# Pre-FFN normalisation and quantisation: statistics taken once for all 16 token tiles, and the rounding moved from VectorE to ScalarE

## The reference

```python
def act_quant(x):
    scale = 127.0 / jnp.clip(jnp.max(jnp.abs(x), axis=-1, keepdims=True), 1e-05)
    return jnp.clip(jnp.round(x * scale), -128, 127) / scale

def _L0_ffn_ref(x, w1, conv_w, conv_b, w2):
    h = bit_linear(x, w1)                      # act_quant(x) @ weight_quant(w1).T
    h = depthwise_conv1d(h.transpose(0, 2, 1), conv_w, conv_b)
    h = jax.nn.silu(h.transpose(0, 2, 1))
    return bit_linear(h, w2)

# x: [16, 2048, 1024] f32, hidden 4096
x = x + _L0_attn_ref(_layernorm(x), ...)
x = x + _L0_ffn_ref(_layernorm(x), w1, conv_w, conv_b, w2)
```

## Time and profile before

| what | value |
|---|---|
| runs of the kernel before | 4776.62 and 4817.77 us, median 4797.2 |
| profiled execution: time | 4801.58 us |
| profiled execution: span of its slowest core (core 0) | 4800.0 us |
| spans of the eight cores | 4755.6 to 4800.0 us |
| busy on core 0: PE / DVE / ACT | 2736.8 / 1853.6 / 964.5 us |
| C-prep of the first sequence on core 0 | 1697.3 to 1819 us |
| C-prep of the second sequence on core 0 | 3802 to 3923 us |

### The profile page before, as it was taken

The page is one execution under the profiler, slowest core; times in us unless marked ns, Lnnn a source line. Parts: engine busy times, 40 slices in busy tenths (PEclk is TensorE's granted clock), DMA queues, the critical chain, the costliest instruction groups (busy, mean ns, idle before and its releaser), DMA issues. The chain is left out here.

```text
span 4800.0 us, 49252 instructions; the slowest of 8 cores (4755.6 to 4800.0 us)
## 1 busy us (share of the span) xinstructions
PE 2736.8 (57%) x16882; PEld 1410.7 (29%) x17064; DVE 1853.6 (39%) x4571; ACT 964.5 (20%) x1070; POOL 45.5 (1%) x68
## 2 busy tenths in 40 slices
PE   0166546677721216768785466456777536768675
PEld 0022113333311114444442122123333224444342
DVE  1121144332323365646554212243222465545643
ACT  0011013455511101111110010025446201101010
POOL 0000000000000000000000000000000000000000
PEclk9999756656555558989898798755665669989888
DMA  7500012111154303444454300000000013544444
GB/s 128 162 27 18 18 68 76 68 62 45 36 156 125 130 9 71 115 136 141 128 153 135 124 19 17 18 18 10 18 18 1 9 27 71 149 114 147 122 136 149
DMA packets 472114, 380.92 MB, mean 79 GB/s; under 512 B 340674, under 2 KB 373570, under 8 KB 466756
## 3 DMA queue, kind: packets, MB, share of 16 engines
q1 hardware_dynamic: 460612, 335.81, 23.9%
q0 software_dynamic: 11264, 41.95, 2.7%
HBM read 335.77 MB, written 41.94 MB: 79 GB/s over the span
## 5 line engine op out<-in xcount | busy, mean ns | idle before, releaser
L80 ACT ACTIVATE b_pt<-b_lp,b_cb 128x1024 bf16<-128x1024 f32 (+3 forms) x640 | 622.9, 985 | 626.2 <-PE b_lp L80 394.7
L80 PE MATMUL c_op<-c_w2b,c_hq 128*128 128x512 bf16 x2032 | 516.8, 400 | 256.3 <-DMA c_w2b<-w2t_s 182.5
L80 PE MATMUL b_av<-V,b_pt 128*128 128x65 bf16 x5120 | 383.7, 241 | 336.6 <-DVE b_pt L80 240.7
L80 PE MATMUL c_hp<-c_xq,c_w1b 128*128 128x257 bf16 x4096 | 525.1, 284 | 66.9 <-ACT c_H L80 58.3
L80 PEld LDWEIGHTS b_av<-V,b_pt 128*128 128x128 bf16 x5120 | 296.9, 125 | 633.5 <-issue 633.5
L80 PEld LDWEIGHTS c_hp<-c_xq,c_w1b 128*128 128x128 bf16 x4096 | 411.2, 101 | 205.3 <-issue 104.6
L80 ACT ACTIVATE c_H<-c_hp,c_cb 128x512 bf16<-128x512 f32 x256 | 175.9, 687 | 1243.3 <-DVE c_H L80 647.2
L80 PE MATMUL b_lp<-Q,K 64*128 64x512 bf16 x1280 | 375.0, 602 | 11.0 <-DVE x L80 9.3
L80 PEld LDWEIGHTS c_op<-c_w2b,c_hq 128*128 128x128 bf16 x2048 | 198.0, 101 | 552.1 <-issue 359.8
L80 DVE TENSOR_TENSOR c_H<-c_hp,c_g1b 128x514 bf16<-128x514 f32 x256 | 176.7, 690 | 462.2 <-PE c_hp L80 462.1
L80 DVE TENSOR_TENSOR b_pt<-b_pt,c_tri 128x128 bf16<-128x128 bf16 x512 | 92.7, 222 | 626.8 <-ACT b_pt L80 626.6
(11 more groups left out here) (119 smaller groups left out, 2256.7 us busy)
## 6 DMA issues: line engine op xcount, KB each, us to landing
c_w2b<-w2t_s SPq DMA_DIRECT2D x256, 512.0 KB, 5.2
c_w1b<-w1t_s SPq DMA_DIRECT2D x128, 512.0 KB, 4.3
pw_stg<-w SPq DMA_DIRECT2D x32, 1024.0 KB, 4.8
wq_stw<-w SPq DMA_DIRECT2D x16, 2048.0 KB, 9.1
a_xt<-x SPq DMA_DIRECT2D x32, 512.0 KB, 3.7
b_xr<-x SPq DMA_DIRECT2D x32, 512.0 KB, 3.5
out<-c_obf POOLq DMA_DIRECT2D x32, 512.0 KB, 3.1
wq_s<-p_wbf POOLq DMA_DIRECT2D x16, 512.0 KB, 8.0
```

The costliest lines, as they stand in the source:

```text
L80: h = getattr(eng, en["name"])(*en["args"], **en["kwargs"])
```

## The change

Everything between the two memsets of c_xq and the barrier is rewritten:

- Statistics are taken for all 16 token tiles before the group loop: 32 `bn_stats` (into the new tile c_pb), 16 `bn_aggr` (c_mw), and one chain of addition, square root, reciprocal and Newton step on 128x16 values of the new tile c_cq instead of four chains on 128x4 values. The new tiles take 1408 bytes of each partition.
- In each group VectorE keeps the four normalisations, the four maxima and the four small steps to the scale. Two waits are added ahead of the normalisations from the second group on (for the transposes and the roundings of the group before); for the transposes it waited before.
- The eight rounding instructions go to ScalarE as `activation` with `AF.Identity`: the first with a 128x1 scale and a 128x1 bias (MAGIC), the second with a 128x1 bias (-MAGIC). They are issued in pairs: first rounding of tiles 0 and 1, a ScalarE drain, second rounding of tiles 0 and 1, then the same for tiles 2 and 3.
- TensorE no longer waits for the whole group's rounding but for that of the one tile (`sc_r2[u]`).

TensorE's instructions are the same in number and order. The diff, cut where the small steps repeat:

```diff
@@ -791,85 +791,104 @@
                 nc.sbuf_tensor(f"c_xv{s}", [128, 4 * D], F32, side="right"))
             cxm = es_cp.enter_context(
                 nc.sbuf_tensor(f"c_xm{s}", [128, 4 * D], BF16, side="right"))
+            cpb = es_cp.enter_context(
+                nc.sbuf_tensor(f"c_pb{s}", [128, 192], F32, side="right"))
+            mv16 = es_cp.enter_context(
+                nc.sbuf_tensor(f"c_mw{s}", [128, 32], F32, side="right"))
+            cs2 = es_cp.enter_context(
+                nc.sbuf_tensor(f"c_cq{s}", [128, 128], F32, side="right"))
             ve.inc(r.vector.memset(
                 xq2.rearrange("p (c t) -> p c t", c=8)[:, :, 0:1], 0.0))
             ve.inc(r.vector.memset(
                 xq2.rearrange("p (c t) -> p c t", c=8)[:, :, S + 1:S + 2], 0.0))
             tn_pq = [0] * NT
             ve_pq = [0] * NT
-            var_s = mvc.rearrange("p (j two) -> p two j", two=2)[:, 1:2, :]
+            sc_r2 = [0] * NT
+            sc_r1 = [0] * NT
+            for u in range(NT):
+                ve.inc(r.vector.bn_stats(cpb[:, u * 12:u * 12 + 6],
+                                         x2[:, u * D:u * D + 512]))
+                ve.inc(r.vector.bn_stats(cpb[:, u * 12 + 6:u * 12 + 12],
+                                         x2[:, u * D + 512:(u + 1) * D]))
+            ve.inc(r.vector.drain())
+            for u in range(NT):
+                ve.inc(r.vector.bn_aggr(mv16[:, u * 2:(u + 1) * 2],
+                                        cpb[:, u * 12:u * 12 + 12]))
+            ve.inc(r.vector.drain())
+            var16 = mv16.rearrange("p (j two) -> p two j", two=2)[:, 1:2, :]
+            ve.inc(r.vector.tensor_scalar_add(
+                cs2.rearrange("p (a b) -> p a b", a=1)[:, :, 0:16], var16,
+                EPS))
+            r.wait(r.scalar, ve)
+            sc.inc(r.scalar.activation(cs2[:, 16:32], cs2[:, 0:16], AF.Sqrt))
+            r.wait(r.vector, sc)
...
+            ve.inc(r.vector.tensor_mul(cs2[:, 64:80], cs2[:, 32:48],
+                                       cs2[:, 48:64]))
+            ve.inc(r.vector.drain())
             for tq in range(NT // 4):
+                q0 = 4 * tq
+                if tq >= 1:
+                    r.wait(r.vector, tn, tn_pq[q0 - 1])
+                    r.wait(r.vector, sc, sc_r1[q0 - 1])
                 for j in range(4):
-                    u = 4 * tq + j
-                    ve.inc(r.vector.bn_stats(bnsc[:, j * 12:j * 12 + 6],
-                                             x2[:, u * D:u * D + 512]))
-                    ve.inc(r.vector.bn_stats(bnsc[:, j * 12 + 6:j * 12 + 12],
-                                             x2[:, u * D + 512:(u + 1) * D]))
-                ve.inc(r.vector.drain())
-                for j in range(4):
-                    ve.inc(r.vector.bn_aggr(mvc[:, j * 2:(j + 1) * 2],
-                                            bnsc[:, j * 12:j * 12 + 12]))
-                ve.inc(r.vector.drain())
-                ve.inc(r.vector.tensor_scalar_add(
-                    cst.rearrange("p (a b) -> p a b", a=1)[:, :, 0:4], var_s,
-                    EPS))
-                r.wait(r.scalar, ve)
-                sc.inc(r.scalar.activation(cst[:, 4:8], cst[:, 0:4], AF.Sqrt))
...
-                if tq >= 1:
-                    r.wait(r.vector, tn, tn_pq[4 * tq - 1])
-                for j in range(4):
-                    u = 4 * tq + j
+                    u = q0 + j
                     ve.inc(r.vector.tensor_scalar(
                         cxt[:, j * D:(j + 1) * D], x2[:, u * D:(u + 1) * D],
-                        mvc[:, 2 * j:2 * j + 1], cst[:, 16 + j:17 + j],
+                        mv16[:, 2 * u:2 * u + 1], cs2[:, 64 + u:65 + u],
                         ALU.subtract, ALU.mult))
                 ve.inc(r.vector.drain())
                 for j in range(4):
-                    ve.inc(r.vector.reduce_max(cst[:, 20 + j:21 + j],
+                    u = q0 + j
+                    ve.inc(r.vector.reduce_max(cs2[:, 80 + u:81 + u],
                                                cxt[:, j * D:(j + 1) * D],
                                                axis=AX.X,
                                                apply_absolute_value=True))
                 ve.inc(r.vector.drain())
...
+                ve.inc(r.vector.tensor_scalar_max(
+                    cs2[:, 96 + q0:100 + q0], cs2[:, 80 + q0:84 + q0], 1e-5))
+                ve.inc(r.vector.drain())
+                ve.inc(r.vector.reciprocal(cs2[:, 112 + q0:116 + q0],
+                                           cs2[:, 96 + q0:100 + q0]))
+                ve.inc(r.vector.drain())
+                ve.inc(r.vector.tensor_single_scalar(
+                    cs2[:, 112 + q0:116 + q0], cs2[:, 112 + q0:116 + q0],
+                    127.0, ALU.mult))
+                ve.inc(r.vector.tensor_scalar(
+                    g1col[:, q0:q0 + 4], cs2[:, 96 + q0:100 + q0],
+                    mw1_bc[:, 0:1], 1.0 / 127.0, ALU.mult, ALU.mult))
+                ve_q = ve.inc(r.vector.drain())
+                r.wait(r.scalar, ve, ve_q)
+                if tq >= 1:
+                    r.wait(r.scalar, tn, tn_pq[q0 - 1])
+                for pj in range(2):
+                    for j in (2 * pj, 2 * pj + 1):
+                        u = q0 + j
+                        sc_r1[u] = sc.inc(r.scalar.activation(
+                            cxt[:, j * D:(j + 1) * D],
+                            cxt[:, j * D:(j + 1) * D], AF.Identity,
+                            scale=cs2[:, 112 + u:113 + u],
+                            bias=magic_bc[:, 0:1]))
+                    sc.inc(r.scalar.drain())
+                    for j in (2 * pj, 2 * pj + 1):
+                        u = q0 + j
+                        sc_r2[u] = sc.inc(r.scalar.activation(
+                            cxm[:, j * D:(j + 1) * D],
+                            cxt[:, j * D:(j + 1) * D], AF.Identity,
+                            bias=nmagic_bc[:, 0:1]))
                 for j in range(4):
-                    ve.inc(r.vector.tensor_scalar(
-                        cxt[:, j * D:(j + 1) * D], cxt[:, j * D:(j + 1) * D],
-                        cst[:, 28 + j:29 + j], MAGIC, ALU.mult, ALU.add))
-                ve.inc(r.vector.drain())
-                for j in range(4):
-                    ve.inc(r.vector.tensor_single_scalar(
-                        cxm[:, j * D:(j + 1) * D], cxt[:, j * D:(j + 1) * D],
-                        -MAGIC, ALU.add))
-                ve_q = ve.inc(r.vector.drain())
-                for j in range(4):
-                    u = 4 * tq + j
-                    r.wait(r.tensor, ve, ve_q)
+                    u = q0 + j
+                    r.wait(r.tensor, sc, sc_r2[u])
                     if not (tq == 0 and j == 0):
                         r.wait(r.tensor, ve, ve_pq[u - 1])
                     for c in range(8):
```

More of the change, by code:

```diff
@@ new lines, in build_program @@
+            r.wait(r.vector, sc)
+            ve.inc(r.vector.reciprocal(cs2[:, 32:48], cs2[:, 16:32]))
+            ve.inc(r.vector.drain())
+            ve.inc(r.vector.tensor_mul(cs2[:, 48:64], cs2[:, 32:48],
+                                       cs2[:, 32:48]))
+            ve.inc(r.vector.drain())
+            ve.inc(r.vector.tensor_mul(cs2[:, 48:64], cs2[:, 48:64],
+                                       cs2[:, 0:16]))
+            ve.inc(r.vector.drain())
+            ve.inc(r.vector.tensor_scalar(cs2[:, 48:64], cs2[:, 48:64],
+                                          -0.5, 1.5, ALU.mult, ALU.add))
@@ L816, in build_program @@
-                r.wait(r.scalar, ve)
-                sc.inc(r.scalar.activation(cst[:, 4:8], cst[:, 0:4], AF.Sqrt))
-                r.wait(r.vector, sc)
-                ve.inc(r.vector.reciprocal(cst[:, 8:12], cst[:, 4:8]))
-                ve.inc(r.vector.drain())
[L821 to L832, removed]
-                if tq >= 1:
-                    r.wait(r.vector, tn, tn_pq[4 * tq - 1])
@@ L847, in build_program @@
                 ve.inc(r.vector.drain())
-                ve.inc(r.vector.tensor_scalar_max(cst[:, 24:28],
-                                                  cst[:, 20:24], 1e-5))
+                ve.inc(r.vector.tensor_scalar_max(
+                    cs2[:, 96 + q0:100 + q0], cs2[:, 80 + q0:84 + q0], 1e-5))
                 ve.inc(r.vector.drain())
-                ve.inc(r.vector.reciprocal(cst[:, 28:32], cst[:, 24:28]))
+                ve.inc(r.vector.reciprocal(cs2[:, 112 + q0:116 + q0],
+                                           cs2[:, 96 + q0:100 + q0]))
@@ L852, in build_program @@
                 ve.inc(r.vector.drain())
[L853 to L859, removed]
```

## The result

The changed kernel took 4763.67 us (median of 31 runs, 4741.85 to 4822.58). The kernel before took 4791.78 us (median of 30 runs). The medians lie 28.1 us apart. The ratio is 0.9937, with a 95% interval of 0.9918 to 0.9956: 30 us less, 21 to 39 by the interval. By the bound of 2% that is the same. The ratio leaves out the slowest run of either kernel (4822.58 and 4851.57 us), which fell in a slower state of the chip. Forecast were 29.9 us less and 4767 us.

The account below looks back on a forecast made before the run. The prediction took C-prep to be bound by VectorE's chain, with nothing of another stage beside it. Its terms, -16.8 and -13.1 us, took 4797.2 to 4767 us, range 4737 to 4802, with 0.97 on within 2%.

Parts of the forecast that it names:

- Term 1: In C-prep, statistics once instead of four times save three small chains of 2.80 us in each sequence: -16.8 us.
- the one opening: In C-prep, from the first bn_stats to the first normalisation, one opening of 24.7 us.
- Term 2: In C-prep, rounding on ScalarE overlapping transposes and copies gains 1.64 us in each of 8 groups: -13.1 us.
- ScalarE can match VectorE's start: In each C-prep group, ScalarE's first rounding can start when VectorE's did, at 1745.37 in the earlier trace.
- What ends last: In each C-prep group, rounding of tile 2, then two times transposes and copy; VectorE goes on at 11.65 us.
- VectorE idle ahead of the copy of tile 0: In each C-prep group VectorE, its queue held at that copy, idles for about 4.7 us.
- The drain: ScalarE's drain between roundings taken as 0.14 us from VectorE's gap; the rival of dear drains, 1.28 us each, had 0.12.
- The sum: Over the whole kernel, -16.8 - 13.1 = -29.9 us, from 4797.2 to 4767 us, -0.6%.
- The clock rival: Stage C's granted clock shifts, some 15 us for 0.01 over both stages; lower gives back the gain 0.11, higher adds 0.10.
- the 875 us of the earlier trace: Stages of 875 us on either side of C-prep were read as TensorE's and untouched by the change.

Follow-up runs that it names:

- e1: The changed kernel with the rounding left on VectorE, so only the statistics change against the kernel before; C-prep 224.9 us, ratio 0.9946 to the kernel before.
- e7: The changed kernel with the second rounding on VectorE tile by tile and no ScalarE drain; C-prep 197.8 us, one run of 4742.02 us.
- e6: The changed kernel with the next group's normalisations and maxima run during ScalarE's rounding, and second buffers; C-prep 156.9 us, ratio 0.9834 to the kernel before.
- e3: The changed kernel with TensorE's transposes waiting for the group's last rounding; C-prep 255.7 us, one run of 4811.04 us.
- e5: The changed kernel with its 32 bn_stats done twice; C-prep 254.4 us, ratio 1.0017 to the kernel before.
- e4: The changed kernel with five ScalarE drains in place of each one; C-prep 221.0 us, one run of 4771.20 us.

## Why the prediction was right

- *Term 1, the statistics, -16.8 us.* Measured alone, 16.1. The mechanism is right, and working on 16 columns cost little: the reciprocal takes 0.25 us for 0.18. The 2.80 us for a chain were read from the second group alone, and it is one of the dear ones. The third group of the kernel before (core 0) shows the other kind:

```profile
1758.66 4.84 DVE L80 BATCH_NORM_STATS2 c_bn<-x 128x6 f32<-128x512 bf16 x8
...
1766.36 2.98 DVE L80 TENSOR_SCALAR c_xv<-x,c_mv,c_st 128x1024 f32<-128x1024 bf16 x4 [0.21 <-issue]
```

Its opening takes 7.70 us, not 8.05. The six later openings are 8.05, 7.70 and 8.05 in the first sequence and 7.70 three times in the second, on every core. By these the six chains are 15.4 us (2 x 2.80 + 4 x 2.45) and not 16.8. Against that, the one opening was foretold as 24.7 us and takes 24.2 (24.5 in the second sequence of the changed kernel). One miss takes 1.4 us off the gain, the other adds some 1.1 to it in e1; that they nearly cancel was luck.
- *Term 2, the rounding, -13.1 us.* Right in its sign and its mechanism, too large in size: measured 9.0 alone and 8.6 on top of term 1 (224.9 less 216.3). Two steps were mis-sized. The roundings were put at 1.15 and 1.11 us and took 1.23 and 1.14, so tile 2's second rounding began 7.05 us behind the first one's start (1773.85 less 1766.80) instead of 6.70. And TensorE's transposes of tile 2 began 0.25 us behind the end of the rounding in seven of the eight groups (0.34 in the group shown) where I had 0.15. Together with 0.03 for the longer last rounding that is 0.5 us in each of 8 groups, 4 of the 4.5 us that were missing. "ScalarE can match VectorE's start" held within 0.1 us: the first rounding began 0.42 us behind c_gc's start, before it was 0.36.
- *What ends last.* "Rounding of tile 2, then two times transposes and copy" is what the rows show in all groups. What the prediction does not say is how close the next chain lies: by its own times tile 2 waits until 7.96 us, where tile 0's transposes and two turns would end at 7.52, and measured it is 0.67 us on average. e7 took 9.2 us off each sequence, of which the early rounding of tile 2 accounts for under 3 and the earlier start of tile 0 for the rest.
- *VectorE idle ahead of the copy of tile 0.* Foretold 4.7 us, 5.20 measured; e6 turns it into time.
- *The drain*, taken at 0.14 from VectorE's rows, is 0.12. By the figure of the Trainium skill ("ScalarE: Activation LUTs", "What ACT_TABLE_LOAD costs"), taken for every drain as an estimate, term 2 would have been a loss; here no explicit drain came near it, so the drain that the Trainium skill gives with a load is not the price of this instruction.
- The formula in the same section of the Trainium skill (280 ns and 0.833 ns for each element with one 128x1 operand, 93 ns for each further one, neighbours overlapping by 93) gives an estimate of 1133 ns for the second rounding and 1226 for the first. The trace agrees: 1140 and 1229, and two of the first kind in a row take 2.37 us, an overlap of 0.09. It would have been the better source for the first rounding than my extrapolated 1.15.
- *The rule to keep additions and multiplications on VectorE* (the Trainium skill, "ScalarE: Activation LUTs", "Rules for kernel authors"). The trace agrees on the price of an instruction (1.23 and 1.14 against 0.75 and 0.69 us). Against the rule the move gained 9 us with the waits by the tile; e3 shows the loss that follows without overlap.
- *The sum.* -29.9 foretold, -24.8 in the stage, -30 (21 to 39) in the ratio. The total met the forecast more closely than its terms did: 4.5 us of term 2 and 0.7 of term 1 were missing, and scatter or the unexplained few microseconds filled them. That closeness is luck. The 4767 set out from 4797.2, the median of two runs; from the 4791.78 of the 30 the same sum gives 4762, again within 4 us of the 4763.67 measured.
- *The clock rival.* C-prep's clock stayed at 0.50, and e5 and e6 moved the mean core span with the stage, to within 5 us, over some 100 us of difference (+8.3 for +13.3, -83.7 for -84.1). One reading of the prediction is off, without weight here: the 875 us of the earlier trace rows are stage C, which stands behind C-prep only; ahead of it come stage B and, in the first sequence, the weights.

## What to carry to other kernels

Moving work from a busy engine to an idle one paid here only for what ran side by side afterwards. Look at what stands next in the queue of the relieved engine: if it waits for the moved work, as the copies did here, put the next group's independent work ahead of it (e6: 59 us less than the changed kernel's C-prep, where the move alone had given 9). Between barriers, where one chain sets a stage, a few microseconds can be forecast from rows and checked by the stage's own length, which here agreed to 0.1 us over eight cores while the total needed 30 runs to show 0.6%.

## What the runs showed of the hardware

- A first ScalarE drain leaves a gap of 0.12 us between two activations of 128x1024, and each further one adds 0.07 us. In the trace of e4 (core 3) the drain instructions themselves have records too: the first of a row lasts 2.36 us, from just behind the start of the pair of roundings to 0.04 us behind their end, and the four further ones last 8 to 14 ns each. So the drain waits beside the work ahead of it, and costs little once that is done.
- From the end of a ScalarE activation to the start of TensorE's transposes that wait for it mostly passed 0.25 us, as for tile 2 of the changed kernel's first group (core 5; 1752.75 + 1.14 to 1754.15):

```profile
1752.75 2.19 ACT L80 ACTIVATE c_xm<-c_xv,c_nmg 128x1024 bf16<-128x1024 f32 x2
...
1754.15 1.01 PE L80 MATMUL c_tp<-c_idb,c_xm 128*128 128x128 bf16 x8 [1.70 <-ACT c_xm L80]
```

It was 0.14 for tile 0 of either sequence's first group, and 0.34 for tile 2 of the second group (1773.85 + 1.14 to 1775.34) and tile 0 of the eighth. The same place has the same figure on all eight cores, so this is not scatter. I had expected one figure; what makes the difference stays open.
- A small chain of the same instructions took 2.80 us in two groups of the kernel before and 2.45 in four, again the same on every core. In the dearer one VectorE stands still for 0.49 us between two multiplications with nothing that the profile shows to wait for:

```profile
1734.82 0.16 DVE L80 TENSOR_TENSOR c_st<-c_st 128x4 f32<-128x4 f32 x1
1735.47 0.16 DVE L80 TENSOR_TENSOR c_st<-c_st 128x4 f32<-128x4 f32 x1 [0.49 <-issue]
```
